# Flamingo-style block: the experts' down projection in three half-precision products

## The chip, the cores and the metric

The kernel runs on one core of one Trainium2 chip. Time is device time in microseconds (us) of one execution, the median of several runs. The engines are TensorE (PE, its weight loads PEld), VectorE (DVE), ScalarE (ACT), GpSimd (POOL) and SyncE (SP, which only issues DMAs here).

## The reference

Two layers on 4096 tokens (64 sequences of 64) of width 128. Each layer is an attention step and then a mixture of experts, each added to x behind a gate:

```
x = x + tanh(g_xattn[0]) * L0_xattn(layernorm(x), ctx)
x = x + tanh(g_ffn[0])   * L0_ffn(layernorm(x))
x = x + tanh(g_xattn[1]) * L1_xattn(layernorm(x), ctx, mask)
x = x + tanh(g_ffn[1])   * L1_ffn(layernorm(x))
```

Layer 0's experts: a router picks the top 2 of 8 experts for a token; for expert e, `h = relu(x @ W1[e] + b1[e])` (128 to 512), `y = h @ W2[e] + b2[e]` (512 to 128), and the two y are added with the router's softmax weights. Layer 1's experts: the 8192 pairs of token and expert are sorted by expert and cut into 8 equal chunks, `h = gelu(x @ w1[e])`, `y = h @ w2[e]`, weighted and added back. Everything is fp32.

## The kernel before

Before each expert stage the tokens' rows are scattered to DRAM (`xs`), sorted by expert. A row holds the normalised token twice in half precision (a high part and the rest, the low part), then its index and its weight. The stage then works through tiles of 256 rows: 40 tiles in layer 0 (an expert's rows are padded to whole tiles) and 32 in layer 1. A round is 8 tiles (`XS_LEAD`). The first and the last round are written out; those between, three in layer 0 and two in layer 1, are a loop with a register for its index. All engines run their own instruction streams and meet by semaphores; buffers and semaphores come in pairs, used by even and odd tiles (`v = q % 2`).

For one tile q:
- SyncE loads two blocks of 128 rows from `xs` (`load_rows`).
- TensorE, `gather`: waits for the rows and transposes them, 4 matmuls of 128x128 in half precision into PSUM (line 929).
- VectorE, `parts`: copies the transposed high and low parts to `xgT` (line 1614).
- TensorE, `up`: 12 matmuls of 256 columns in half precision (line 758, as for all matmuls by `mm`). w1 was split before into `w1h` and `w1l`, scaled by 256 (`WSCALE`); the three products w1h x high, w1h x low and w1l x high are added in PSUM.
- ScalarE, `step`: in layer 0 four Relu activations with a bias (line 1195), in layer 1 one Gelu of 128x1024 (line 1198), out of PSUM to `hid` in fp32, times 1/256.
- TensorE, `down`: for each half u of the tile (128 rows) four fp32 matmuls, with 128 columns of `hid` as weights and the expert's `w2` moving (lines 947 to 950). An fp32 matmul is recorded as two passes.
- VectorE, `result`: waits for y; in layer 0 it loads the expert's number (line 1626) and adds b2; then two multiplications by the rows' weights (line 1632) write `yrow`.
- GpSimd, `step`: a tiny operation `turn` (line 526), then two indirect DMAs that scatter the rows to `ys` (line 528).

The order on TensorE is gather(q+1), up(q), down(q-1); on VectorE parts(q+1), result(q-1). Each instruction stream is in order. Which expert a tile belongs to is known at run time only: `expert(tile)` on TensorE (line 954) loads it from SBUF into a register before each up and each down projection, and the addresses in `w1h`, `w1l` and `w2` are computed from that register by operations of TensorE's sequencer. In the profile these are `PEldq TENSOR_LOAD`, `PEldq FUSED_REGOPS` and `PEldq ALU_OP`; the operations for a matmul's address carry the matmul's line, 758. ScalarE and VectorE load it too in layer 0 (lines 1193 and 1626).

`w2` is loaded once in each layer. In layer 1 the first six tiles are gathered by GpSimd's indirect DMAs (`head_gathered`), the later ones by SyncE.

Of the kernel before, what the change touches and what calls it, by code (L numbers as in the profile page):

```python
# [11 lines left out]
ALU = mybir.AluOpType  # L12
# [9 lines left out]
P = 128  # L22
# [47 lines left out]
def build(nc, A, out):  # L70

    ctx = ExitStack()
    with ctx:
# [154 lines left out]
        hid = at(10.25, [2, FC, TILE])  # L228
        yrow = at(18.5, [XS_LEAD, 2, D])
# [30 lines left out]
        def banks(b, n):  # L260
# [21 lines left out]
              for l in range(2)]  # L282
# [8 lines left out]
        w2_in = sem("w2_in")  # L291
# [5 lines left out]
               ("stored", XS_LEAD), ("biased", 1))}  # L297
# [156 lines left out]
        def _(pool):  # L454
# [41 lines left out]
            g.memset(g32, 0.0)  # L496
# [257 lines left out]
        def _(pe):  # L754
# [157 lines left out]
            def experts(l):  # L912
                f, i0 = ff, before[l]
                pe.wait_ge(w1_lo[l], E)
                if l == 1:
                    pe.wait_ge(w2_in, 16)
# [25 lines left out]
                def down(i, q, e):  # L942
                    v, m = q % 2, (i + i0) * (XS_LEAD // 2) + q // 2
                    pe.wait_ge(f["hid"][v], m + 1)

                    wait(pe, f["yrow"][v], m)
                    for u in range(2):
                        for c in range(FC):
                            ins = mm(PS[:, 6 + v, u * D:(u + 1) * D], hid[:, v, c, u * P:(u + 1) * P],
                                     w2[:, ds(e * FF + c * D, D)], start=c == 0, stop=c == FC - 1)  # L950
                    ins.then_inc(f["y"][v], 1)
# [172 lines left out]
        def _(act):  # L1124
# [58 lines left out]
            def experts(l):  # L1183
                f, i0 = ff, before[l]
                act.wait_ge(table, l + 1)
                act.wait_ge(w_late, 16 * NL)
                def step(i, q):
                    v, m = q % 2, (i + i0) * (XS_LEAD // 2) + q // 2
                    act.wait_ge(f["up"][v], m + 1)
                    wait(act, f["y"][v], m)  # L1190
                    b = 2 + 2 * v
                    if l == 0:
                        e = act.value_load(eidx_i[0:1, l, ds(i * XS_LEAD + q, 1)], min_val=0, max_val=E - 1)
                        for c in range(FC):
                            ins = a.activation(hid[:, v, c, :], PF[:, b * 512 + c * TILE:b * 512 + (c + 1) * TILE],  # L1195
                                               ACT.Relu, bias=b1[:, ds(e * FC + c, 1)], scale=1 / WSCALE)
                    else:
                        ins = a.activation(hid[:, v, :, :].rearrange("p c n -> p (c n)"), banks(b, 1024),  # L1198
                                           ACT.Gelu, scale=1 / WSCALE)
                    ins.then_inc(f["hid"][v], 1)  # L1200

                expert_tiles(act, l, step)
# [84 lines left out]
        def _(dve):  # L1287
# [54 lines left out]
            def load(c):  # L1342
# [5 lines left out]
                if c == 0:  # L1348
# [6 lines left out]
                    dve.wait_ge(gates, 1)  # L1355
                    v_.tensor_copy(wqqa[:, 0:H], PS[:, 4, 0:H])
# [250 lines left out]
            def experts(l):  # L1607
# [9 lines left out]
                def result(i, q):  # L1617
# [3 lines left out]
                    if not (isinstance(i, int) and i + i0 == 0):  # L1621
                        dve.wait_ge(f["turn"][0], (i + i0 - 1) * XS_LEAD + q + 1)
                        dve.wait_ge(f["stored"][q], (i + i0) * STORED)
# [10 lines left out]

                def round_(i, first, last):
                    for q in range(XS_LEAD):
                        if q < XS_LEAD - 1:
# [3 lines left out]
                        if q >= 1:  # L1641
                            result(i, q - 1)
                        elif not first:
                            result(i - 1, XS_LEAD - 1)
# [6 lines left out]
                round_(rounds_ - 1, False, True)  # L1651
                result(rounds_ - 1, XS_LEAD - 1)

# [10 lines left out]
            dve.wait_ge(x1_done, NC)  # L1664
            v_.memset(kmask[:, 0, :, :, :], 0.0).then_inc(k_blank, 1)
# [76 lines left out]
            route_table(1)  # L1742
            experts(1)
# [50 lines left out]
```

## Time and profile before

| | |
|---|---|
| median of 3 runs | 770.82 us (767.83 to 771.95) |
| profiled execution, own time | 765.61 us |
| its span | 763.8 us |
| mean granted TensorE clock | 0.795 of full speed |
| PE busy | 518.3 us, 68% of the span |
| PEld busy | 428.3 us, 56% |
| DVE busy | 416.7 us, 55% |
| ACT busy | 235.4 us, 31% |
| POOL busy | 339.5 us, 44% |
| chain that ended last | PE 50%, DVE 24%, POOL 8%, issue 8%, DMA 6% |
| of it, PE on line 758 | 46% |

The span is the time from the first to the last instruction of the program in the profile. The chain that ended last is followed back from the last instruction, at each step to what released it. Shares of busy time are averages over stages with different limits: the expert stages lie at about 205 to 350 us (layer 0) and 614 to 740 us (layer 1).

### The profile page before, as it was taken

How to read it: one execution, taken by the hardware profiler on the slowest of the kernel's cores; microseconds unless marked ns; L12 is line 12 of the kernel's file. 1: busy time of each engine (PE TensorE's matmuls, PEld its weight loads, DVE VectorE, ACT ScalarE, POOL GpSimd, SP SyncE). 2: the span in 40 equal slices, each digit the busy share in tenths (PEclk: the TensorE clock that was granted, in tenths of full speed). 3: DMA queues.
4: the chain of work that ended last, by engine and by line, in shares of the span. 5: the costliest groups of instructions: out<-in, count | busy, mean ns of one | idle time of the engine just before them, and what ended most of it. 6: DMA issues, size and time to landing. Idle time of an engine off the chain costs nothing.

```text
span 763.8 us, 17097 instructions
## 1 busy us (share of the span) xinstructions
PE 518.3 (68%) x5273; PEld 428.3 (56%) x5274; DVE 416.7 (55%) x1454; ACT 235.4 (31%) x411; POOL 339.5 (44%) x424
## 2 busy tenths in 40 slices
PE   1587958423199999992387687777862076999950
PEld 1255745301199899991254466666651065989950
DVE  4785686987123333334895377878568611222215
ACT  0221011222044444443621365454631021232310
POOL 6212106777345656665500000071647676666650
PEclk9978876755599999997565599696765578999995
DMA  7911101124222222342763265353214123232219
GB/s 210 264 32 42 28 1 44 51 95 129 69 72 79 76 79 73 80 136 76 236 187 124 55 162 151 96 150 71 67 45 147 45 54 101 80 79 80 68 52 317
DMA packets 73194, 76.51 MB, mean 100 GB/s; under 512 B 12984, under 2 KB 61368, under 8 KB 73064
## 3 DMA queue, kind: packets, MB, share of 16 engines
q1 hardware_dynamic: 58504, 50.98, 24.4%
q0 software_dynamic: 10224, 22.40, 9.5%
q10 hardware_dynamic: 4400, 2.26, 1.0%
q8 instruction: 40, 0.66, 0.4%
q14 instruction: 26, 0.21, 0.1%
HBM read 46.15 MB, written 29.34 MB: 99 GB/s over the span
## 4 chain that ended last, share of the span: by engine, by line
PE 50%; DVE 24%; POOL 8%; issue 8%; DMA 6%; ACT 2%; SPq 1%; POOLq 0%; ACTq 0%; DVEq 0%
PE PS L758 46%; POOL xs L517 5%; DVE XN L1323 3%; DVE stats L1302 3%; DMA work<-ys 3%; DVE X L1297 2%; PE PS L929 2%; DVE work L1712 2%; DVE work L1297 1%; POOL work L565 1%; DVE rtmp L1297 1%; DVE mv L1305 1%; DVE nwt L1297 1%; PE PS L1074 1%; DMA work<-max_rows 1%
## 5 line engine op out<-in xcount | busy, mean ns | idle before, releaser
L517 POOL DMA_INDIRECT xs<-pack,adr_i x80 | 78.7, 983 | 197.8 <-ACT pack L1147 142.0
L528 POOL DMA_INDIRECT ys<-work x144 | 140.7, 977 | 34.5 <-issue 34.5
L758 PE MATMUL PS<-w,work 128*128 x1152 | 143.8, 279 | 3.0 <-issue 1.7
L758 PEld LDWEIGHTS PS<-w,work 128*128 128x128 f32 x1152 | 134.9, 193 | 9.0 <-issue 6.8
L758 PE MATMUL PS<-work,w1h 128*128 128x256 f16 x576 | 103.1, 281 | 1.1 <-issue 1.1
L1195 ACT ACTIVATE work<-PS,b 128x256 f32<-128x256 f32 x160 | 62.7, 474 | 95.5 <-PE PS L758 69.2
L1297 DVE TENSOR_TENSOR work<-PS,work 128x256 f32<-128x256 f32 (+3 forms) x82 | 33.0, 405 | 94.7 <-issue 55.6
L758 PE MATMUL PS<-work 97*64 97x256 f16 (+5 forms) x608 | 74.0, 318 | 15.4 <-DVE work L1429 7.6
L758 PE MATMUL PS<-work,w1l 128*128 128x256 f16 x288 | 80.9, 281 | 0.0
L758 PEld LDWEIGHTS PS<-work 97*64 97x64 f16 (+2 forms) x608 | 56.0, 163 | 25.9 <-DVE work L1429 10.9
L1632 DVE TENSOR_SCALAR work<-PS,work 128x128 f32<-128x128 f32 x64 | 19.5, 346 | 79.0 <-PE PS L758 79.0
L929 PE MATMUL PS<-ident,work 128*128 128x128 f16 x288 | 29.5, 228 | 47.2 <-DMA work<-xs,headadr_i 24.6
L758 PEld LDWEIGHTS PS<-work,w1h 128*128 x576 | 54.7, 101 | 8.4 <-issue 2.1
L1712 DVE TENSOR_REDUCE work<-PS 128x16 f32<-128x1024 f32 x32 | 39.1, 1222 | 33.8 <-PE PS L758 33.8
L1198 ACT ACTIVATE work<-PS 128x1024 f32<-128x1024 f32 x32 | 32.8, 1024 | 80.2 <-PE PS L758 80.1
L758 PE MATMUL PS<-work,W 128*128 128x512 f32 x60 | 48.4, 933 | 8.1 <-DVE work L1297 3.4
L517 POOL DMA_INDIRECT xs<-work,adr_i x48 | 47.1, 981 | 14.8 <-issue 13.6
L1614 DVE COPY work<-PS 128x512 f16<-128x512 f16 x72 | 30.1, 418 | 39.7 <-PE PS L929 39.5
L929 PEld LDWEIGHTS PS<-ident,work 128*128 128x128 f16 x288 | 22.8, 102 | 50.7 <-issue 39.6
L526 POOL TENSOR_TENSOR turn<-lane 1x1 f32<-1x1 f32 x72 | 17.3, 240 | 72.6 <-DVE work L1632 72.4
L1236 ACT ACTIVATE XN<-PS,mask_bias 128x1024 f32<-128x1024 f32 x32 | 35.6, 1113 | 19.1 <-PE PS L758 18.9
L758 PE MATMUL PS<-ident,work 128*64 128x36 f32 x512 | 25.9, 255 | 22.7 <-DVE work L1297 22.7
(259 smaller groups left out, 809.8 us busy)
## 6 DMA issues: line engine op xcount, KB each, us to landing
work<-xs SPq DMA_DIRECT2D x132, 65.0 KB
work<-ys SPq DMA_DIRECT2D x12, 512.0 KB, 5.9
k_parts<-work SPq DMA_DIRECT2D x24, 128.0 KB
w<-k_parts SPq DMA_DIRECT2D x8, 384.0 KB
work<-k_parts SPq DMA_DIRECT2D x32, 96.0 KB
work<-q_parts SPq DMA_DIRECT2D x8, 384.0 KB
work<-q_parts SPq DMA_DIRECT2D x32, 96.0 KB
ys<-work POOLq DMA_INDIRECT x144, 2.3
```

The lines of the kernel that those rows point to most:

```text
L517: g.indirect_dma_start(xs[l], bass.IndirectOffsetOnAxis(adr_i[:, k, T:T + 1], 0), pack_of(l, c)[:, s, k, :].bitcast(U32), None)\
L528: g.indirect_dma_start(ys[l], bass.IndirectOffsetOnAxis(xin[:, q, u, :].bitcast(U32)[:, D:D + 1], 0), yrow[:, q, u, :], None).then_inc(ff[ ...
L758: return t.matmul(o, lhsT, rhs, start=start, stop=stop, skip_group_check=True)
L929: ins = t.transpose(o[:, h, u, :], xin[:, q, u, h * D:(h + 1) * D], ident16[:])
L1195: ins = a.activation(hid[:, v, c, :], PF[:, b * 512 + c * TILE:b * 512 + (c + 1) * TILE], ACT.Relu, bias=b1[:, ds(e * FC + c, 1)], scale=1 ...
L1198: ins = a.activation(hid[:, v, :, :].rearrange("p c n -> p (c n)"), banks(b, 1024), ACT.Gelu, scale=1 / WSCALE)
L1236: a.activation(pexp[:, T % 2, :], banks(2, 1024), ACT.Exp, bias=mask_bias[:, T:T + 1]).then_inc(p_done, 1)
L1297: return v_.tensor_tensor(o, x, y, op)
L1302: ins = v_.bn_stats(stats[:, T, :], X[:, T, 0:D])
L1323: ins = v_.tensor_scalar(XN[:, slot + s, :], X[:, T, 0:D], mv[:, T, 0:1], rstd[:, T:T + 1], ALU.subtract, ALU.mult)
L1614: v_.tensor_copy(xgT[:, v, :, :].rearrange("p h n -> p (h n)"), PS[:, v, 0:TILE].bitcast(F16))\
L1712: v_.tensor_reduce(rmaxq[:, c % 2, s, :], banks(0, 1024).rearrange("p (h k) -> p h k", h=H), AX, ALU.max).then_inc(s_max, 1)
```

## The change

The down projection is made like the up projection. `w2` is split into a high and a low half-precision part, times 256, in `w2_parts` (which lies over `XN`): the high parts by ScalarE, 8 copies of 128x512, the low parts by VectorE, 8 operations (`split_w2`), before each expert stage. Behind its activation ScalarE writes `hid_hi`, a half-precision copy of `hid`, in one activation of 128x1024. VectorE makes `hid_lo` = hid - hid_hi in two halves of a tile, 128x512 each (`low`). The down projection has 24 matmuls of 128 columns in half precision: for each half u 8 with `hid_hi` (high and low weights), then, behind a wait for that half of the low part, 4 with `hid_lo` and the high weights. The factor 1/256 goes into the gates' columns `gt[:, 2:4]`, and b2 is multiplied by 256.

VectorE's order in a round becomes result(q-2), parts(q+1), low(q-1); in layer 1's first round low(3) comes before parts(5). ScalarE waits for the low part of tile q-2 before it writes `hid` again, and for the down projection of q-2 before it writes `hid_hi`. The semaphore `turn` starts at 8. The wait for w2 in layer 1 moves from TensorE to ScalarE.

```diff
+        hid_hi = at(48, [2, FC, TILE], F16)
+        hid_lo = at(68, [2, FC, TILE], F16)
+        w2_parts = XN[:].rearrange("p t d -> p (t d)").bitcast(F16)
...
-            g.memset(g32, 0.0)
+            g.memset(g32, 0.0).then_inc(ff["turn"][0], XS_LEAD)
...
                 def down(i, q, e):
-                    v, m = q % 2, (i + i0) * (XS_LEAD // 2) + q // 2
-                    pe.wait_ge(f["hid"][v], m + 1)
+                    v, m, tile = q % 2, (i + i0) * (XS_LEAD // 2) + q // 2, (i + i0) * XS_LEAD + q
+                    if q == 0 and isinstance(i, int) and i == 0:
+                        pe.wait_ge(w2_lo, (l + 1) * E)
+                    pe.wait_ge(f["hi"][0], tile + 1)
 
                     wait(pe, f["yrow"][v], m)
                     for u in range(2):
+                        o = PS[:, 6 + v, u * D:(u + 1) * D]
                         for c in range(FC):
-                            ins = mm(PS[:, 6 + v, u * D:(u + 1) * D], hid[:, v, c, u * P:(u + 1) * P],
-                                     w2[:, ds(e * FF + c * D, D)], start=c == 0, stop=c == FC - 1)
+                            for part in range(2):
+                                mm(o, hid_hi[:, v, c, u * P:(u + 1) * P],
+                                   w2_parts[:, ds(e * 2 * FF + part * FF + c * D, D)], start=c + part == 0, stop=False)
+                        pe.wait_ge(f["lo"][0], 2 * tile + u + 1)
+                        for c in range(FC):
+                            ins = mm(o, hid_lo[:, v, c, u * P:(u + 1) * P],
+                                     w2_parts[:, ds(e * 2 * FF + c * D, D)], start=False, stop=c == FC - 1)
                     ins.then_inc(f["y"][v], 1)
...
             def experts(l):
                 f, i0 = ff, before[l]
+                act.wait_ge(w_late, 16 * NL)
+                act.wait_ge(pack_lo, (l + 1) * NC)
+                if l == 1:
+                    act.wait_ge(w2_in, 16)
+                for e in range(E):
+                    a.activation(w2_parts[:, e * 2 * FF:e * 2 * FF + FF], w2[:, e * FF:(e + 1) * FF], ACT.Copy,
+                                 scale=WSCALE).then_inc(w2_hi, 1)
                 act.wait_ge(table, l + 1)
...
                 def step(i, q):
                     act.wait_ge(f["up"][v], m + 1)
-                    wait(act, f["y"][v], m)
+                    if not isinstance(i, int) or tile >= 2:
+                        act.wait_ge(f["lo"][0], 2 * tile - 2)
...
                     ins.then_inc(f["hid"][v], 1)
+                    act.wait_ge(f["hid"][v], m + 1)
+                    wait(act, f["y"][v], m)
+                    a.activation(hid_hi[:, v, :, :], hid[:, v, :, :], ACT.Copy).then_inc(f["hi"][0], 1)
...
+                    v_.tensor_scalar(gt[:, 2:4], gt[:, 2:4], 1 / WSCALE, None, ALU.mult)
...
+                def low(i, q):
+                    v, m = q % 2, (i + i0) * (XS_LEAD // 2) + q // 2
+                    dve.wait_ge(f["hi"][0], (i + i0) * XS_LEAD + q + 1)
+                    wait(dve, f["y"][v], m)
+                    for u in range(2):
+                        half = slice(u * P, (u + 1) * P)
+                        tt(hid_lo[:, v, :, half], hid[:, v, :, half], hid_hi[:, v, :, half], ALU.subtract)
+                            .then_inc(f["lo"][0], 1)
+
                 def round_(i, first, last):
                     for q in range(XS_LEAD):
+                        if q >= 2:
+                            result(i, q - 2)
+                        elif not first:
+                            result(i - 1, XS_LEAD + q - 2)
+                        late = first and l == 1 and q == HEAD0 - 1
+                        if late:
+                            low(i, q - 1)
                         if q < XS_LEAD - 1:
                             parts(i, q + 1)
                         elif not last:
                             parts(i + 1, 0)
                         if q >= 1:
-                            result(i, q - 1)
+                            if not late:
+                                low(i, q - 1)
                         elif not first:
-                            result(i - 1, XS_LEAD - 1)
+                            low(i - 1, XS_LEAD - 1)
...
+            def split_w2(l):
+                for e in range(E):
+                    hi, lo = (w2_parts[:, (2 * e + part) * FF:(2 * e + part + 1) * FF] for part in range(2))
+                    dve.wait_ge(w2_hi, l * E + e + 1)
+                    v_.scalar_tensor_tensor(out=lo, in0=w2[:, e * FF:(e + 1) * FF], scalar=WSCALE, in1=hi,
+                                            op0=ALU.mult, op1=ALU.subtract).then_inc(w2_lo, 1)
...
             dve.wait_ge(x1_done, NC)
+            dve.wait_ge(w_late, 16 * NL)
+            split_w2(0)
+            v_.tensor_scalar(b2b, b2b, WSCALE, None, ALU.mult)
...
             route_table(1)
+            split_w2(1)
             experts(1)
```

## Rows read from the trace of the kernel before

**Rows 1.** Busy time by stretch, both loops (us, PE, PEld, DVE, ACT, POOL, PEclk, DMA share, GB/s)

```profile
235.00:318.00 83.00, 81.95 (x768) 76.09 (x768) 29.95 (x96) 37.51 (x97) 50.96 (x73) 1.00 0.29 77
653.00:708.00 55.00, 54.47 (x514) 50.84 (x514) 15.13 (x48) 16.37 (x16) 34.05 (x49) 1.00 0.29 78
```

**Rows 2.** Line 929's transposes, two stretches (count: ns min/median/max, first and last start)

```profile
L929 PE MATMUL PS<-ident,work x98: 218/220/220, 235.0 to 318.3; 128*128 128x128 f16 x98
...
L929 PE MATMUL PS<-ident,work x65: 218/220/220, 653.0 to 708.0; 128*128 128x128 f16 x65
```

**Rows 3.** TensorE in order of time, one tile of layer 0 (start, us, engine, line)

```profile
299.39 0.27 PE L758 MATMUL PS<-work,w1l 128*128 128x256 f16 x1
...
299.50 1.97 PE L758 MATMUL PS<-w,work 128*128 x16
...
301.31 0.39 PE L929 MATMUL PS<-ident,work 128*128 128x128 f16 x4
...
302.84 1.95 PE L758 MATMUL PS<-w,work 128*128 x16
...
304.63 0.39 PE L929 MATMUL PS<-ident,work 128*128 128x128 f16 x4
```

**Rows 4.** TensorE's sequencer by line, five successive stretches from 299.3 to 303.0

```profile
L758 PEldq FUSED_REGOPS  x4: 46/46/46, 299.3 to 299.7; - x4
...
L954 PEldq TENSOR_LOAD <-eidx_i x1: 304/304/304, 300.1 to 300.1; - x1
...
L758 PEldq FUSED_REGOPS  x4: 46/46/46, 300.9 to 301.6; - x4
...
L954 PEldq TENSOR_LOAD <-eidx_i x1: 302/302/302, 301.8 to 301.8; - x1
...
L758 PEldq FUSED_REGOPS  x4: 46/46/46, 302.6 to 303.0; - x4
```

**Rows 5.** TensorE in order of time, layer 1's first tiles (idle before, and releaser)

```profile
636.57 0.40 PE L929 MATMUL PS<-ident,work 128*128 128x128 f16 x4 [2.45 <-DMA work<-xs,headadr_i]
640.33 0.61 PE L929 MATMUL PS<-ident,work 128*128 128x128 f16 x4 [3.36 <-DMA work<-xs]
```

**Rows 6.** TensorE's sequencer, line 954, from 639.0 to 640.6

```profile
L954 PEldq TENSOR_LOAD <-eidx_i x1: 395/395/395, 640.3 to 640.3; - x1
```

**Rows 7.** ScalarE and VectorE in order of time, the same tile of layer 0

```profile
300.41 1.57 ACT L1195 ACTIVATE work<-PS,b 128x256 f32<-128x256 f32 x4 [1.76 <-PE PS L758]
...
302.49 0.42 DVE L1297 TENSOR_TENSOR work<-PS,work 128x256 f32<-128x256 f32 x1 [2.02 <-issue]
...
303.35 0.42 DVE L1614 COPY work<-PS 128x512 f16<-128x512 f16 x1
```

**Rows 8.** VectorE in order of time, before each expert stage

```profile
182.39 1.28 DVE L1297 TENSOR_TENSOR work<-PS,work 128x512 f16<-128x512 f32 x2
...
205.24 0.42 DVE L1614 COPY work<-PS 128x512 f16<-128x512 f16 x1 [12.64 <-PE PS L929]
...
614.22 0.42 DVE L1614 COPY work<-PS 128x512 f16<-128x512 f16 x1 [8.51 <-PE PS L929]
```

**Rows 9.** TensorE and VectorE in order of time, one tile of layer 1

```profile
643.84 2.71 PE L758 MATMUL PS<-w,work 128*128 x16
...
646.59 0.61 DVE L1632 TENSOR_SCALAR work<-PS,work 128x128 f32<-128x128 f32 x2 [5.20 <-PE PS L758]
...
647.12 0.42 DVE L1614 COPY work<-PS 128x512 f16<-128x512 f16 x1
```

**Rows 10.** Groups by line (count, busy us, mean ns of one, idle before)

```profile
L528 POOL DMA_INDIRECT ys<-work x144 | 140.7, 977 | 34.5 <-issue 34.5
...
L1147 ACT ACTIVATE pack<-pack 128x1024 f16<-128x1024 f16 x10 | 10.3, 1049 | 5.1 <-DVE pack L1297 5.1
```

**Rows 11.** Busy time by stretch, two in layer 1's attention (columns as in rows 1)

```profile
452.00:456.00 4.00, 2.19 (x61) 1.64 (x57) 3.00 (x6) 2.33 (x4) 0.00 (x0) 1.00 0.80 142
520.00:580.00 60.00, 41.46 (x714) 33.17 (x704) 41.51 (x174) 26.14 (x50) 25.68 (x27) 0.70 0.32 85
```

More of the change, by code:

```diff
@@ L290, in build @@
         w1_in = [[sem(f"w1_in{l}_{u}") for u in range(2)] for l in range(2)]
-        w2_in = sem("w2_in")
+        w2_in, w2_hi, w2_lo = sem("w2_in"), sem("w2_hi"), sem("w2_lo")
         pack_hi, pack_lo = sem("pack_hi"), sem("pack_lo")
@@ L296, in build @@
               (("xin", XS_LEAD), ("xT", 2), ("xT_sb", 2), ("up", 2), ("hid", 2), ("y", 2), ("yrow", 2), ("turn", 1),
-               ("stored", XS_LEAD), ("biased", 1))}
+               ("stored", XS_LEAD), ("biased", 1), ("hi", 1), ("lo", 1))}
         rounds = [TILES[l] // XS_LEAD for l in range(2)]
@@ L914, in experts @@
                 pe.wait_ge(w1_lo[l], E)
-                if l == 1:
-                    pe.wait_ge(w2_in, 16)
                 pe.wait_ge(table, l + 1)
@@ L1184, in experts @@
                 f, i0 = ff, before[l]
+                act.wait_ge(w_late, 16 * NL)
[5 more added lines that the diff above has]
+                                 scale=WSCALE).then_inc(w2_hi, 1)
                 act.wait_ge(table, l + 1)
-                act.wait_ge(w_late, 16 * NL)
                 def step(i, q):
-                    v, m = q % 2, (i + i0) * (XS_LEAD // 2) + q // 2
+                    v, m, tile = q % 2, (i + i0) * (XS_LEAD // 2) + q // 2, (i + i0) * XS_LEAD + q
                     act.wait_ge(f["up"][v], m + 1)
-                    wait(act, f["y"][v], m)
+                    if not isinstance(i, int) or tile >= 2:
+                        act.wait_ge(f["lo"][0], 2 * tile - 2)
                     b = 2 + 2 * v
@@ L1621, in result @@
                     if not (isinstance(i, int) and i + i0 == 0):
-                        dve.wait_ge(f["turn"][0], (i + i0 - 1) * XS_LEAD + q + 1)
+                        dve.wait_ge(f["turn"][0], (i + i0) * XS_LEAD + q + 1)
                         dve.wait_ge(f["stored"][q], (i + i0) * STORED)
@@ L1633, in result @@
                     ins.then_inc(f["yrow"][v], 1)
+                def low(i, q):
[4 more added lines that the diff above has]
+                        half = slice(u * P, (u + 1) * P)
+                        tt(hid_lo[:, v, :, half], hid[:, v, :, half], hid_hi[:, v, :, half], ALU.subtract)                            .then_inc(f["lo"][0], 1)
                 def round_(i, first, last):
                     for q in range(XS_LEAD):
+                        if q >= 2:
[5 more added lines that the diff above has]
+                            low(i, q - 1)
                         if q < XS_LEAD - 1:
@@ L1651, in experts @@
                 round_(rounds_ - 1, False, True)
+                result(rounds_ - 1, XS_LEAD - 2)
+                low(rounds_ - 1, XS_LEAD - 1)
                 result(rounds_ - 1, XS_LEAD - 1)
+            def split_w2(l):
[4 more added lines that the diff above has]
+                                            op0=ALU.mult, op1=ALU.subtract).then_inc(w2_lo, 1)
             def combine(l, c):
```

## The prediction

> **What bounds the kernel now.** I read the expert stages alone, since both layers' down projections lie there. First the busy time by stretch: in the loops TensorE is busy for 81.95 of 83 us in layer 0 and 54.47 of 55 in layer 1, at a granted clock of 1.00 [rows 1]. Then the transposes that open each tile, four to a tile: 24 tiles of layer 0's loop take 83.2 us (235.0 to 318.2), 3.47 us each, and the 16 of layer 1 take 55.0 (653.0 to 708.0), 3.44 each [rows 2]. Then one tile in the order of time [rows 3]: transposes and the up projection (12 matmuls) from 301.31 to 302.84, the down projection from 302.84 to the next transposes at 304.63. So the array's turn is 1.53 + 1.79 = 3.32 us, and the reader sees no hole in it.
>
> A page of busy time can't show the second limit. The rows of TensorE's sequencer [rows 4] are of register work alone: four address operations for a down projection (299.3 to 299.7), a load of the expert's number at 300.1, the operations of an up projection (of eight, the four FUSED_REGOPS are shown, from 300.9), a load at 301.8, the next down's first operation at 302.6. That is 3.3 us for a tile (I take 3.27). The views show nothing that it waits for in between, so the sequencer is about as full as the array. A register operation takes about 0.12 us of it: four starts span 0.4 us with their matmuls between. The matmuls themselves are cheap in it: between the last address operation at 299.7 and the load at 300.1 lie five matmuls, four transposes, a wait and an operation, so a matmul costs at most 0.03. And the sequencer stops at a wait: at 640.33 a transfer releases the transposes [rows 5], and the load behind them in the program starts at 640.3 and not before [rows 6].
>
> **The change, part by part.** *The array.* Eight fp32 matmuls, recorded as 16 passes, take 1.79 us. 24 matmuls of 128 columns in half precision replace them. The nearest row is the four transposes, of the same shape and type and each with its weights loaded: they take 0.39 us with the last one's 0.22 [rows 2, 3], so they start 0.056 apart, and 24 take 1.34. The turn falls from 3.32 to 2.87. Bounds: 0.056 a matmul, and the 0.11 of a pass (1.79 / 16) if loading weights showed beside so short a stream: 2.7 us, a turn of 4.2.
> The Trainium skill, "TensorE: Matmul & The Clock Gate", section "Back-to-back issue gap", gives about 81 ns for a matmul of 128 columns in a stream of loads and matmuls. By it the down projection would take 1.94 us and the turn would be 3.47. The trace has 56 ns, but for four in a row only.
>
> *TensorE's sequencer.* The weights' offset hangs on the expert's register. Today four address operations serve eight matmuls, since the second half of a tile uses the four again. Now there are eight offsets (two parts, four chunks), used again by the low products and by the second half: 4 more operations, 0.48 us. The 16 more matmuls cost 0 to 0.5 at 0.03 each; I take 0.1, since nine matmuls and other work fit into 0.4 above. In the loops the thresholds of the waits differ from tile to tile, one for "hi" and two for "lo": three operations of about 0.1, 0.3. Sum: 3.27 + 0.48 + 0.1 + 0.3 = 4.15, say 4.2 us. In the first and last rounds, which are written out, indices and thresholds are constants, and I estimate 3.75. Bounds: nothing (3.3, all of it cached and free), and an operation for each of the 24 matmuls (4.2 + 16 x 0.12 = 6.1). These turns don't run ahead of anything: the wait for the last low part stops the sequencer, and gather, two loads, the up projection and the next down come behind it.
>
> *VectorE's ring.* low(q-1) stands behind result(q-2) and parts(q+1); result(q-2) needs down(q-2), and down(q-1) needs low(q-1): one turn a tile. In layer 0 the down projection ends at 299.50 + 1.97 = 301.47, but the add of the bias starts at 302.49, since the expert's number is loaded behind the wait; the copy of parts ends at 303.35 + 0.42 = 303.77 [rows 3, 7]. That is 2.30. Two subtractions of 128x512 come on: a pair of such operations takes 1.28 [rows 8], and as VectorE's records overlap by 0.08 I count 1.20. Then a semaphore and the last four matmuls, 0.39 as for four transposes [rows 3] and 0.1 for the first load: 0.53. The turn is 2.30 + 1.20 + 0.53 = 4.03 us. In layer 1 the down ends at 643.84 + 2.71 = 646.55 and the copy at 647.12 + 0.42 = 647.54 [rows 9]: 0.99 + 1.20 + 0.53 = 2.72 us. The subtraction has one fp32 and one half-precision input from SBUF. Bounds: the 0.42 of the half-precision copy of 512 [rows 7], which makes layer 0's turn 3.5, and the pair's 0.69 each, which I take as the nearer in type.
>
> *ScalarE* gets a copy of 128x1024, 1.05 [rows 10], behind 1.57 of activations, which start at 300.41, 0.75 behind the last up matmul (299.39 + 0.27) because of its own load [rows 3, 7]: 3.4, under the 4.0. *GpSimd* issues two scatters of 0.98 for a tile [rows 10], some 2.6 with the gaps: hidden. *The split of w2* is 8 copies on ScalarE and 8 operations of about 0.6 on VectorE, 5 us in each layer, and the scaling of b2 about 1. VectorE is idle for 12.64 us before layer 0's first copy and 8.51 before layer 1's [rows 8], which hides them; without that cover they cost 6 and 5. The scaling of two gate columns is one small operation, 0.2 at most.
>
> *The sum,* against the profiled run's 765.6 us. What today's periods have above the array's turn, at most 0.15 (3.47 against 3.32: the branch, late loads), I add to the longest new turn in the loops: 4.35. Layer 0: 24 x (4.35 - 3.47) = +21.1. Layer 1: 16 x (4.35 - 3.44) = +14.6. Tiles of written-out rounds: 12 in layer 0 at VectorE's 3.95 (its load has less to compute there) against some 3.37, +7; 9 in layer 1 at 3.85 against some 3.4, +4. Filling layer 0's pipeline and draining both: a copy of 1.05 and subtractions of 1.2 come on, less 0.45 of down projection, 3 x 1.8 = +5.4. Layer 1's first tiles run into waits for transfers that end at 636.57 and 640.33 [rows 5]; of the 2.8 us or so that they lose I count 0.4. Together +52.5: 818.1. The median of the runs shown is 5.2 above the profiled run (770.8 against 765.6): about 822 us, that is 823.3 rounded towards the near rivals.
>
> **The rivals.**
> 1. *The array alone is the limit.* Register work and semaphores hide, the turn is 2.87, and 61 tiles save 0.45 or so each: 27.5 us, less the 5.4 of the ends: 770.8 - 22 = 749. For it: rows 1 and 3 show an array without holes. Against it: rows 4, whose turn is 3.3 by itself. It decides from the point where the mean turn falls below some 3.4. This is the faster case.
> 2. *VectorE's ring without the sequencer.* If the sequencer's additions are half of what I think or less, layer 0 runs at 4.03 + 0.1 and layer 1 at 3.4 as now: 24 x 0.66 + 12 x 0.58 + 6 = +29, about 800. If its turn goes below the array's, layer 1 gains some 10 (790), and the subtraction's lower bound takes 36 x 0.5 = 18 from layer 0 (772).
> 3. *Short matmuls run slower in a stream than in fours.* Halfway between the bounds, at 0.083 each and with nothing else new, the turn is 1.53 + 2.0 = 3.5: 61 x 0.18 + 5.4 = +16, about 787. Beneath a sequencer's turn of 4.2 it changes nothing. The figure of "TensorE: Matmul & The Clock Gate" in the Trainium skill, above, would come out here.
> 4. *An address operation for every matmul.* 61 x 1.9 above the forecast, about 938. Against it: four serve eight today.
> 5. *The clock falls.* The array would be busy 2.87 of 4.2 us, 68%. A stretch with 2.19 of 4 busy has a clock of 1.00, while one with 41.46 of 60 has 0.70, there with long holes [rows 11]. Mine are near 1.3 us and regular. At 1.2 GHz the turn is 5.7: 61 x 1.4 more, about 907.
>
> **How the numbers follow.** Forecast 0.63, rival 1 0.07, rival 2 0.19, rival 3 0.04, rival 4 0.04, rival 5 0.03. The range goes from 780, low in rival 2, to 850 (turns of 4.8 in the loops, with 16 matmuls at 0.03 and late loads), and leaves out rivals 1, 4 and 5 and thin ends, under 0.2. A difference within 0.5% can't be told from none here. Faster 0.08 (rival 1 and the bottom of 2), the same 0.03, slower 0.89.
>
> **What would show it.** The transposes of successive tiles 4.2 to 4.4 us apart in both loops, the clock near 1.00, TensorE busy about 70%; eight FUSED_REGOPS for each down projection; VectorE waiting little before its result in layer 0 and over 1 us in layer 1. If layer 1's tiles come 3.3 us apart or less, the sequencer's price is wrong; if layer 0's do, the ring is wrong too. Subtractions of other than 0.69 us, or half-precision matmuls more than 0.06 apart where nothing waits, would shift the terms above.

## The result, and the profile after

The changed kernel takes 821.13 us (median of 4 runs, 815.88 to 824.47), the kernel before beside it 771.38 (4 runs). The ratio is 1.0648, 95% interval 1.0573 to 1.0724: 6.5% slower. The profiled run is of 815.88 us with a span of 813.7, against 765.61 and 763.8 before, so 49.9 us of span have to be found. Of all the runs told below one stands apart: the kernel with fewer thresholds took 1553.8 us in one of its six executions, which no row explains, and its median without it is 817.2 us. In the changed kernel the transposes are on line 930, the matmuls' helper on 761, VectorE's two-tensor helper on 1317, the expert's load on 963.

Busy time by stretch, both loops (columns as in rows 1):

```profile
242.00:328.00 86.00, 75.52 (x798) 58.95 (x796) 47.95 (x119) 51.67 (x100) 49.00 (x61) 1.00 0.23 63
694.00:740.00 46.00, 40.20 (x419) 31.39 (x419) 23.29 (x55) 21.84 (x22) 26.63 (x33) 1.00 0.22 59
```

TensorE was busy for 99% of these stages [rows 1]; now it is for 87 to 88%. That is more than the array's work: a matmul's record is longer (0.22 us) than its place in the stream (0.056 us), so matmuls that start one by one count in full. By the distance of the starts the array has work for 2.87 us of 4.31, 67%. The clock is still 1.00. The transposes that open the tiles, with the first and last start in a window (as in rows 2), of the first loop, the second loop, and the last written-out tiles:

```profile
L930 PE MATMUL PS<-ident,work x100: 218/219/227, 242.9 to 346.5; 128*128 128x128 f16 x100
...
L930 PE MATMUL PS<-ident,work x66: 218/219/220, 684.7 to 753.8; 128*128 128x128 f16 x66
...
L930 PE MATMUL PS<-ident,work x27: 218/219/220, 753.7 to 777.5; 128*128 128x128 f16 x27
```

The 24 tiles of layer 0 take 103.5 us, 4.31 each (before 3.47), the 16 of layer 1 take 69.0, 4.31 each (before 3.44). Six written-out tiles take 23.6, 3.94 each. What fills a tile of layer 1 is on TensorE's sequencer. Four lines of it within one turn, 734.8 to 739.1 (the first is of the down projection alone, to 735.85):

```profile
L761 PEldq FUSED_REGOPS  x8: 46/46/60, 734.8 to 735.7; - x8
...
L956 PEldq FUSED_REGOPS  x1: 42/42/42, 735.8 to 735.8; - x1
L956 PEldq ALU_OP  x1: 32/32/32, 736.0 to 736.0; - x1
...
L963 PEldq TENSOR_LOAD <-eidx_i x2: 303/306/308, 736.3 to 738.2; - x2
...
L947 PEldq ALU_OP  x1: 32/32/32, 738.8 to 738.8; - x1
```

There are eight address operations, 0.12 us apart, where four were [rows 4]; two thresholds for "lo" (line 956) and one for "hi" (line 947); and two loads of the expert's number (line 963). TensorE and VectorE in order of time there:

```profile
734.91 2.06 PE L761 MATMUL PS<-XN,work 128*128 x24 [0.33 <-issue]
736.81 0.39 PE L930 MATMUL PS<-ident,work 128*128 128x128 f16 x4
...
739.15 0.48 PE L761 MATMUL PS<-XN,work 128*128 x3 [0.35 <-issue]
```
```profile
732.91 0.61 DVE L1653 TENSOR_SCALAR work<-PS,work 128x128 f32<-128x128 f32 x2 [1.98 <-PE PS L761]
...
733.77 1.28 DVE L1317 TENSOR_TENSOR work<-work 128x512 f16<-128x512 f32 x2
737.01 0.61 DVE L1653 TENSOR_SCALAR work<-PS,work 128x128 f32<-128x128 f32 x2 [1.96 <-PE PS L761]
```

TensorE has holes put down to "issue", and VectorE waits 1.96 us for it: layer 1's turn, 734.91 to 739.15, is the sequencer's. In layer 0 VectorE is in it too:

```profile
300.39 0.42 DVE L1317 TENSOR_TENSOR work<-PS,work 128x256 f32<-128x256 f32 x1 [1.93 <-PE PS L761]
300.85 0.48 DVE L1653 TENSOR_SCALAR work<-work 128x128 f32<-128x128 f32 x2
301.24 0.42 DVE L1635 COPY work<-PS 128x512 f16<-128x512 f16 x1
301.58 1.28 DVE L1317 TENSOR_TENSOR work<-work 128x512 f16<-128x512 f32 x2
304.44 0.42 DVE L1317 TENSOR_TENSOR work<-PS,work 128x256 f32<-128x256 f32 x1 [1.57 <-PE PS L761]
```
```profile
L345 PEldq EVENT_SEMAPHORE  x1: 51/51/51, 302.9 to 302.9; - x1
...
L963 PEldq TENSOR_LOAD <-eidx_i x1: 303/303/303, 303.2 to 303.2; - x1
```

The second subtraction ends at 301.58 + 1.28 = 302.86; TensorE's sequencer passes its next wait at 302.9 and starts the load behind it at 303.2. In layer 1 the load comes 1.2 us after the subtraction instead (736.3, against 733.77 + 1.28 = 735.05). VectorE's turn from result to result is 304.44 - 300.39 = 4.05 us here. It is one of the short ones: the next takes 4.39, and the loop's turns go from 4.01 to 4.79 round the mean of 4.31.

### The profile page after: what moved, and what is told of

The parts are those of the page before. It is cut to its first block, busy times and chain, and to the rows that moved or that the text cites. A ratio compares the mean times of both kernels' runs of the same rounds, so it can differ in the third digit from the quotient of the medians.

```text
span 813.7 us, 19014 instructions
## 1 busy us (share of the span) xinstructions
PE 538.4 (66%) x5849; PEld 411.4 (51%) x5850; DVE 512.9 (63%) x1616; ACT 319.4 (39%) x499; POOL 367.6 (45%) x424
## 4 chain that ended last, share of the span: by engine, by line
PE 50%; DVE 24%; issue 10%; POOL 6%; DMA 6%; ACT 1%; SPq 1%; DVEq 0%; POOLq 0%; ACTq 0%
PE PS L761 46%; POOL xs L520 3%; DVE XN L1343 3%; DVE stats L1322 3%; DMA work<-ys 2%; DVE X L1317 2%; PE PS L930 2%; DVE work L1317 2%; DVE work L1761 2%; DVE rtmp L1317 1%; POOL work L568 1%; DVE mv L1325 1%; DVE nwt L1317 1%; PE PS L1083 1%; POOL work L575 1%
## 5 line engine op out<-in xcount | busy, mean ns | idle before, releaser
L761 PE MATMUL PS<-XN,work 128*128 (+1 forms) x2752 | 174.1, 232 | 27.2 <-issue 22.7
L531 POOL DMA_INDIRECT ys<-work x144 | 165.1, 1146 | 34.3 <-issue 34.3
L761 PEld LDWEIGHTS PS<-XN,work 128*128 128x128 f16 (+1 forms) x2752 | 137.6, 103 | 72.6 <-issue 54.5
L1317 DVE TENSOR_TENSOR work<-work 128x512 f16<-128x512 f32 (+2 forms) x160 | 100.8, 667 | 6.2 <-ACT work L1220 5.6
L1220 ACT ACTIVATE work<-work 128x1024 f16<-128x1024 f32 x72 | 76.1, 1057 | 2.3
L761 PEld LDWEIGHTS PS<-work,w1h 128*128 x576 | 51.9, 100 | 26.2 <-issue 18.9
L930 PEld LDWEIGHTS PS<-ident,work 128*128 128x128 f16 x288 | 19.8, 101 | 49.6 <-issue 42.2
```

Source lines behind the costliest of these rows:

```text
L531: g.indirect_dma_start(ys[l], bass.IndirectOffsetOnAxis(xin[:, q, u, :].bitcast(U32)[:, D:D + 1], 0), yrow[:, q, u, :], None).then_inc(ff[ ...
L761: return t.matmul(o, lhsT, rhs, start=start, stop=stop, skip_group_check=True)
L930: ins = t.transpose(o[:, h, u, :], xin[:, q, u, h * D:(h + 1) * D], ident16[:])
L1220: a.activation(hid_hi[:, v, :, :], hid[:, v, :, :], ACT.Copy).then_inc(f["hi"][0], 1)
L1317: return v_.tensor_tensor(o, x, y, op)
```

## The experiments

Twelve kernels, in three sets, each with runs of the kernel before on the same chip (median 767.6, 767.1 and 767.2 us). The table has each ratio to these, which can differ by 0.2% from the quotient of the medians. The changed kernel was timed beside the kernel before in its own set only, so it is compared with the others by its ratio, and by its tiles. From each profiled run the table has the mean tile in the two loops (start of tile 9's transposes to tile 33's, and 49's to 65's) and in the last written-out tiles (33 to 39, 65 to 71).

| kernel | us | ratio [95%] | loop 0 | loop 1 | written out 0 / 1 |
|---|---|---|---|---|---|
| before | | 1 | 3.47 | 3.44 | 3.42 / 3.37 |
| changed | 821.1 | 1.065 [1.057, 1.072] | 4.31 | 4.31 | 4.21 / 3.94 |
| constant address | 790.7 | 1.031 [1.025, 1.037] | 4.00 | 3.19 | 3.90 / 3.11 |
| early load on VectorE | 814.9 | 1.062 [1.057, 1.068] | 4.21 | 4.32 | 3.97 / 3.94 |
| one load | 799.0 | 1.043 [1.036, 1.050] | 4.14 | 3.80 | 4.03 / 3.34 |
| one load + early load | 790.0 | 1.031 [1.025, 1.037] | 3.90 | 3.78 | 3.82 / 3.36 |
| the same + ScalarE's early | 784.8 | 1.021 [1.014, 1.029] | 3.72 | 3.78 | 3.59 / 3.36 |
| one subtraction | 834.8 | 1.086 [1.079, 1.094] | 4.52 | 4.23 | 4.41 / 3.92 |
| fewer thresholds | 817.6 | 1.068 [1.062, 1.073] | 4.27 | 4.08 | 4.19 / 3.87 |
| expert from the number | 771.5 | 1.003 [1.000, 1.007] | 3.71 | 3.00 | 3.59 / 2.87 |
| all edits | 767.7 | 1.001 [0.998, 1.005] | 3.66 | 2.98 | 3.59 / 2.87 |
| before, one load | 764.9 | 0.998 [0.994, 1.002] | 3.35 | 3.36 | 3.32 / 3.32 |
| before, third load | 810.1 | 1.058 [1.050, 1.065] | 4.13 | 4.14 | 4.08 / 4.00 |
| before, number | 763.6 | 0.995 [0.992, 0.999] | 3.35 | 3.32 | 3.32 / 3.32 |

**Constant address.** The down projection's weights stand at a fixed address, one load less. This kernel leaves out the choice of the expert there (every tile takes expert 0's `w2`):

```
-    w2_parts[:, ds(e * 2 * FF + part * FF + c * D, D)]      (and the same for the low part)
+    w2_parts[:, part * FF + c * D:part * FF + c * D + D]
-    down(i, q - 1, expert(i * XS_LEAD + q - 1))
+    down(i, q - 1, 0)
...
```

> The changed kernel, but every down projection uses expert 0's weights: its expert load and its eight address operations on TensorE's sequencer are gone, the 24 matmuls and all waits stay. Theory (sequencer sets layer 1, VectorE's ring sets layer 0): the sequencer's turn falls by 8 x 0.12 + 0.75 us; layer 1's tiles come some 2.95 us apart (array 2.87), layer 0's stay at the ring's 4.0 to 4.1; about 787 us against 821. Rival A (24 short matmuls run slowly on the array): layer 1 stays at 4 us or more, 815 us or more. Rival B (the chain activation, copy, subtraction sets both layers): no tile moves, 821 us.

+24 us against the kernel before instead of +50. Layer 1 falls to 3.19 us a tile, below the kernel before's 3.44, with all 24 matmuls in place: what the change cost there is address work and loads, not matmuls. (2.95 was expected; what holds it at 3.19 is open.) Layer 0 stops at 4.00, and there VectorE's ring is alone in charge:

```profile
294.06 0.42 DVE L1317 TENSOR_TENSOR work<-PS,work 128x256 f32<-128x256 f32 x1 [1.49 <-PE PS L761]
...
298.03 0.42 DVE L1317 TENSOR_TENSOR work<-PS,work 128x256 f32<-128x256 f32 x1 [1.49 <-PE PS L761]
```

Every turn from result to result in this loop is between 3.94 and 4.08 us, with 1.47 to 1.60 between the last subtraction and the next result. The forecast's 0.53 for the semaphore and the last matmuls and 1.02 from there to the add (302.49 - 301.47) are 1.55.

**Early load on VectorE.** The load of the expert's number in `result` goes ahead of the wait for y:

```
+    if l == 0:
+        e = dve.value_load(eidx_i[0:1, l, ds(i * XS_LEAD + q, 1)], ...)
     dve.wait_ge(f["y"][v], m + 1)
...
     if l == 0:
-        e = dve.value_load(eidx_i[0:1, l, ds(i * XS_LEAD + q, 1)], ...)
```

> The changed kernel, but VectorE loads the expert's number of layer 0 before it waits for y, not behind the wait. Theory: the ring of layer 0 falls from 4.03 to some 3.3 us, but the sequencer's 4.2 stands beside it in the loops, and its 3.8 in the written-out rounds; only 3 to 6 us are gained, about 817 us, layer 1 unmoved. Rival B (VectorE's ring alone sets layer 0, the sequencer nothing): 0.75 us on each of 38 tiles, 28 us, about 793.

Layer 0's loop gains 0.10, its written-out tiles 0.24. VectorE's ring alone isn't the bound: its rival had 0.75 a tile.

**One load.** TensorE keeps the register from up(q) for down(q). At the first tile of a round, where the down projection is of the round before, it still loads twice:

```
-    up(i, q, expert(i * XS_LEAD + q))
+    e = expert(i * XS_LEAD + q)
+    up(i, q, e)
     if q >= 1:
-        down(i, q - 1, expert(i * XS_LEAD + q - 1))
+        down(i, q - 1, e_before)
...
+    e_before = e
```

> The changed kernel, but TensorE loads the expert's number once a tile (kept in its register from the up projection to the down projection) and not twice. Theory: the sequencer's turn falls by some 0.7 us to 3.5; layer 1's tiles come 3.5 to 3.6 us apart (from 4.23), layer 0's stop at the ring's 4.05; about 799 us. Rivals A (array) and B (VectorE's ring or the chain of activations alone): no change, 821 us.

As expected in time. Layer 1 gains 0.51 of the 0.7 us in the loop and 0.60 outside; layer 0, which VectorE holds too, 0.17. Turn by turn its trace is plainer than its mean: from result to result, 20 of the loop's 23 turns take 3.96 to 4.21 us, most of them 3.96 to 4.03, as with the constant address, and three, one to a round, where the second load is left, take 4.9 to 5.2.

**One load and early load,** both edits:

> Both edits together: one load a tile on TensorE, and VectorE's load before its wait. Theory: two limits side by side in layer 0, so the two together give more than the sum of each alone; layer 0 at 3.5 to 3.6 us a tile, layer 1 at 3.5 to 3.6; about 781 us. If only one of the two limits existed, the time would be that of the better single edit.

790 and not 781: layer 0 gives 0.41 a tile, more than the two apart (0.10 + 0.17), but stops at 3.90. A third ring was under it. ScalarE, its load (line 1212 on its sequencer), then TensorE, of this kernel:

```profile
267.99 1.57 ACT L1214 ACTIVATE work<-PS,b 128x256 f32<-128x256 f32 x4 [1.25 <-DVE work L1319]
269.59 1.06 ACT L1222 ACTIVATE work<-work 128x1024 f16<-128x1024 f32 x1
```
```profile
L1212 ACTq TENSOR_LOAD <-eidx_i x1: 277/277/277, 267.4 to 267.4; - x1
```
```profile
266.89 0.27 PE L761 MATMUL PS<-work,w1l 128*128 128x256 f16 x1
267.00 1.96 PE L761 MATMUL PS<-XN,work 128*128 x24
...
270.80 2.09 PE L761 MATMUL PS<-XN,work 128*128 x24
```

The up projection ends at 267.16, the activations start 0.83 later, the copy to half precision ends at 270.65, and the down projection of the same tile starts at 270.80: 3.64 us. The profile puts the 0.83 down to VectorE, but ScalarE's load of the expert's number starts at 267.4, right behind the up projection's end, and the activations behind that. In the 3.64 us TensorE does one turn's work (down, transposes, up), so they bound the turn: the down projections here start 3.80 apart.

**The same with ScalarE's load early** (its `value_load` goes ahead of the wait for up):

> The changed kernel with one expert load a tile on TensorE and with the loads of VectorE and ScalarE in layer 0 put ahead of their waits for TensorE (the earlier run had the first two of these; it was 22 us slower than the kernel before). Theory (what kept that run's layer 0 at 3.90 us was the chain TensorE's up projection, ScalarE's load of 0.7 us, its activations 1.57, its copy 1.06, then TensorE's next down projection, 3.6 us with the semaphores, with one up projection a turn): without the load the chain is 2.9 us and the sequencer sets the turn as in layer 1, 3.78 in the loop and about 3.45 in the written-out rounds: 24 x 0.12 + 12 x 0.37 = 7 us less, 15 us slower than the kernel before, between 12 and 18. Rival (the sequencer or VectorE held layer 0): no change from that run, 20 to 24 us slower than the kernel before.

Layer 0 falls from 3.90 to 3.72 in the loop and from 3.82 to 3.59 outside, while layer 1, where ScalarE loads nothing, stays at 3.78 and 3.36. The third ring is shown.

**One subtraction** for the whole tile in place of two halves, one wait:

```
-    pe.wait_ge(f["lo"][0], 2 * tile + u + 1)
+    if u == 0:
+        pe.wait_ge(f["lo"][0], 2 * tile + 2)
...
-    for u in range(2):
-        half = slice(u * P, (u + 1) * P)
-        tt(hid_lo[:, v, :, half], ...).then_inc(f["lo"][0], 1)
+    tt(hid_lo[:, v, :, :], hid[:, v, :, :], hid_hi[:, v, :, :], ALU.subtract).then_inc(f["lo"][0], 2)
```

> The changed kernel with one edit: the low part of a tile is made by one subtraction of 512 elements a partition, not by two of 256, and TensorE waits for it once, after the first half's products with the high part, so one threshold less is worked out by its sequencer. Theory (the sequencer sets the turn, the halves buy nothing): 0.16 to 0.3 us less of the sequencer's 4.15 us, of which layer 0 keeps a part because VectorE's ring, 4.0 us, stands just under it: 16 x 0.2 in layer 1's loop, 9 x 0.1, and 24 x 0.15 in layer 0's: 7 us less than the changed kernel, 43 us slower than the kernel before, between 39 and 49. Rival (the halves matter: the array waits for the whole low part 0.6 us longer, and VectorE's ring of result, low part and down projection grows by it): 0.3 to 0.6 us more in each of layer 0's tiles, 12 to 24 us slower than the changed kernel.

Theory and rival were each right in one layer. Layer 1, the sequencer's, gains 0.08 a tile; layer 0, VectorE's, loses 0.21. TensorE and then VectorE in layer 0:

```profile
283.28 1.19 PE L761 MATMUL PS<-XN,work 128*128 x8 [0.29 <-issue]
284.76 1.07 PE L761 MATMUL PS<-XN,work 128*128 x16 [0.29 <-DVE work L1318]
```
```profile
283.49 1.22 DVE L1318 TENSOR_TENSOR work<-work 128x1024 f16<-128x1024 f32 x1
```

16 matmuls wait for the subtraction's end at 284.71, where only the last four would. The halves of the change are worth their price. But 36 x 0.2 - 16 x 0.08 is 6 us, and this kernel's median is 18 us above what the changed kernel's ratio gives (767.1 x 1.065 = 817). The profiled runs lie further apart than the medians, 24.7 us of span (838.4 against 813.7). Of these, 11 us lie between the layers and 5 ahead of layer 0's first transposes (211.4 against 206.2), where nothing was edited. The stretch between the layers:

```profile
388.00:667.00 279.00, 165.89 (x2444) 127.95 (x2444) 193.86 (x668) 111.94 (x176) 90.19 (x85) 0.69 0.39 111
```
```profile
375.00:643.00 268.00, 159.74 (x2446) 125.07 (x2445) 193.51 (x671) 112.07 (x177) 88.51 (x85) 0.71 0.41 116
```

The first row is of this kernel, the second of the changed one: the same instructions, a mean clock of 0.69 against 0.71, and 11 us. From the last tile of layer 0 to the first of layer 1, the profiles here have 272 to 285 us. Whether the end of layer 0 sets how this stretch fares wasn't tried. So I read small edits by their tiles.

**Fewer thresholds.** A semaphore for each half, all three waits on tile + 1:

```
-    pe.wait_ge(f["lo"][0], 2 * tile + u + 1)
+    pe.wait_ge(f["lo"][u], tile + 1)
...
```

> The changed kernel with one edit: the low part's two halves count in two semaphores, so that the three waits of a down projection (high part, first and second half of the low part) have one threshold, tile + 1, and TensorE's sequencer works out one number a tile where it worked out three. Nothing else moves. Theory (the sequencer sets layer 1's turn; in layer 0 VectorE's ring stands at 4.0 us just under it): 0.25 us less in layer 1's loop, 4.05, and 0.1 to 0.2 less in layer 0's, 4.15; 16 x 0.25 + 24 x 0.15 = 8 us less than the changed kernel, 42 us slower than the kernel before, between 38 and 47. Rival (the ring through VectorE or the matmuls set the turn): no change, 50 us slower.

By its tiles the theory held: 0.23 in layer 1's loop (0.25 expected), 0.04 in layer 0's, where the sequencer then waits for VectorE. The time doesn't show it: the tiles give 24 x 0.04 + 16 x 0.23 = 4.6 us, and the stretch between the layers was 5 us longer in this profile.

**The expert from the tile's number,** in layer 1, on top of the three loads' edits (each expert has four tiles there):

```
 def expert(tile, of=None):
+    if l == 1:
+        return of[0] * (XS_LEAD // 4) + of[1] // 4
...
```

> The kernel with one expert load a tile on TensorE and early loads on VectorE and ScalarE (18 us slower than the kernel before), with one more edit: in layer 1, where the tile's number gives its expert, TensorE's sequencer works the expert out from the number and loads nothing. Theory (the sequencer sets layer 1's turn, 3.78 us in the loop and 3.36 outside it; without the load it is 3.0, and the array's 2.87 us of matmuls with a short gap behind them comes next): 3.2 in the loop, 3.1 outside, 16 x 0.55 + 9 x 0.25 = 11 us less, 7 us slower than the kernel before, between 3 and 11. Rival (VectorE or ScalarE holds layer 1): no change, 18 us slower than the kernel before.

Layer 1's loop falls to 3.00 us (3.2 was expected), and outside it, where nothing is left for the sequencer to compute, the array's own turn is laid open:

```profile
717.01 0.39 PE L930 MATMUL PS<-ident,work 128*128 128x128 f16 x4
...
718.54 1.50 PE L761 MATMUL PS<-XN,work 128*128 128x128 f16 x24
719.88 0.39 PE L930 MATMUL PS<-ident,work 128*128 128x128 f16 x4
```

1.53 + 1.34 = 2.87 us, 0.056 for each of 24 matmuls. This is the forecast's turn of the array, to the hundredth.

**All edits together:** one load a tile, the early loads on VectorE and ScalarE, layer 1's expert from the tile's number, and fewer thresholds.

> All edits that took instructions from TensorE's sequencer or from the chains of layer 0, together: one expert load a tile, early loads on VectorE and ScalarE, layer 1's expert from the tile's number, one threshold for the three waits. Theory (layer 0: the sequencer, 3.72 us in the loop, falls to 3.45, below it lies VectorE's ring of 3.3; layer 1: the array's 2.87 us, 3.0 to 3.1 measured as a turn, below before's 3.44): 24 x 0.25 + 16 x 0.15 less than the kernel without the thresholds' edit, so about 1 us faster than the kernel before, between 6 faster and 5 slower. Rival (the array's work in the changed kernel is not less than before's): 10 us or more slower than the kernel before.

1 us faster was expected, 1 us slower came, and the interval (-0.2 to +0.5%) holds no difference: a tie, with the changed kernel's 24 matmuls a tile. Layer 1's tiles are now 0.46 shorter than before's, layer 0's still 0.19 longer. There, in some tiles, the sequencer stops 0.6 us at the wait for the second half, and load, addresses and the next up projection come behind it. And the turn in which a round's second load is left takes 4.3 to 4.9 us, where the others take 3.25 to 3.87.

**The kernel before, one load; a third load; number.** The mirror: the same instructions taken from or added to the kernel before. The third load is one line, `expert(i * XS_LEAD + q)`, ahead of up.

> The kernel before, with one edit: the register with a tile's expert number is loaded once a tile on TensorE (nine loads for eight tiles) and kept for the down projection, instead of twice. Theory (array and sequencer nearly tied before, 3.32 us and 3.27 us a tile, and what one gives the other does not take at once: the sequencer's second load falls where the array has emptied its queue): the loops' 3.47 and 3.44 us go down to the array's 3.3, 40 tiles x 0.15 = 6 us, the written-out rounds keep 3.3 to 3.4; about 6 us faster than the kernel before, between 3 and 9. Rival (the array alone sets the tile's turn before): no change, within 1.5 us. Rival (sequencer alone): the loops fall by the whole 0.7 us a tile or to 2.9: 20 us or more faster.

> The kernel before, with one edit: a third load of the tile's expert number on TensorE's sequencer in each tile, whose value nobody uses. Theory (the sequencer is next to the array and becomes the bound when 0.7 us of instructions are added): 3.27 + 0.7 = 4.0 us a tile in the loops and about 3.7 in the written-out rounds: 24 x 0.53 + 16 x 0.56 + 28 x 0.3 = 30 us slower than the kernel before, between 22 and 38. Rival (the sequencer is hidden behind the array, and the changed kernel is slower for other reasons, its ring through VectorE and its matmuls): within 5 us of the kernel before.

> The kernel before with the same two savings on TensorE's sequencer: one expert load a tile in layer 0, none in layer 1. It leaves the array as the bound, 3.32 us a tile. Theory: 24 x 0.12 + 16 x 0.1 = 4.5 us less than the kernel before, between 1 and 7; layer 1's turn is 3.32 us, since nothing is left to take from the array. Rival (the sequencer held the loops of layer 1 by itself): 3.2 us or less a tile there, 8 us or more faster than the kernel before.

The third load costs 0.66 and 0.70 us a tile in the loops, and 43 us in all. Its theory had 30 and at most 38, with 0.3 for a written-out tile, but those slow by 0.63 to 0.66 as well. Its loop of layer 1:

```profile
L929 PE MATMUL PS<-ident,work x67: 218/219/220, 676.2 to 742.7; 128*128 128x128 f16 x67
```

(16 tiles in 66.3 us.) So before, the sequencer stood right under the array, as rows 4 had it. Taking a load away gives 0.12 and 0.08 a tile and ends just above the array's 3.32, at 3.35 and 3.36. In time 6 us were expected of it, and its 2.2 us can't be told from no change. With layer 1's loads gone too, the loop there is 3.32:

```profile
L929 PE MATMUL PS<-ident,work x67: 219/219/219, 652.9 to 706.2; 128*128 128x128 f16 x67
```

This version is the fastest of all, 0.5% under the kernel before (interval 0.1 to 0.8%).

## Why the prediction was right, step by step

822 us was forecast against 821.1 measured. The mechanism was right. That the number is right to 1 us is in part luck: the sum went by the profiled run, 818.1 against 815.9, in which two misses of some 3 us cancel (below), and that the median lies 5.2 above the profiled run again is chance.

- *The array,* 2.87: shown, in the kernel with the expert from the number. Rival 1 (749 us) fell: the array's turn is what it said, and the sequencer doesn't let it through. Rival 3 fell: a stream of 24 keeps 0.056. The Trainium skill's 81 ns ("TensorE: Matmul & The Clock Gate", section "Back-to-back issue gap") isn't what this trace has, and the measurement decides.
- *The sequencer,* 4.15 to 4.2: eight address operations and three thresholds, as forecast; 4.24 in the turn shown above. Its price was tested from both sides: a load taken away or added moves a tile by 0.5 to 0.7, three thresholds made one by 0.23 (some 0.12 each, 0.1 was taken). Rival 4 (an operation for each matmul) fell by the x8.
- *VectorE's ring,* 4.03 in layer 0: 4.05 in the turn shown. Subtractions cost 0.68 to 0.69 us each, as taken from the pair in rows 8. With the sequencer relieved (constant address) the whole loop runs at 4.00. In layer 1 it was forecast at 2.72: VectorE's result, copy and subtractions take 735.05 - 732.91 = 2.14, with the forecast's 0.53 for the semaphore and the last matmuls 2.67, and it idles 1.96 us before the next result.
- *Which of the two bounds layer 0.* The forecast took the longer and added 0.15. They are coupled, as I read it: the sequencer stops for VectorE's second half, then runs its own work, and VectorE waits for what this leads to. Relieving one gives 0.10 or 0.17, both 0.41, and then ScalarE's ring, which the forecast had at 3.4 without the semaphores and which has 3.64 with them, stands next. Rival 2 would have had VectorE's ring in charge and no more. It fell for the changed kernel, since the sequencer holds layer 1 and has its share in layer 0, but its state of layer 0 can be had: with the address operations and a load gone (constant address) every turn there is VectorE's, and with one load gone most are.
- *The clock* (rival 5) stayed at 1.00 in both loops.
- *Hidden work.* The splits of w2 took 4.91 and 4.90 us, beside an idle VectorE. The first:

```profile
188.07 4.91 DVE L1697 SCALAR_TENSOR_TENSOR XN<-w,XN 128x512 f16<-128x512 f32 x8
...
206.83 0.42 DVE L1635 COPY work<-PS 128x512 f16<-128x512 f16 x1 [8.85 <-PE PS L930]
```

Whether they are hidden wholly isn't shown for layer 0. In the four profiles of the kernel before and its variants the first transposes start at 202.5 to 204.7 us, in the ten with the splits at 204.0 to 211.4, 2.9 later in the mean, and no run took the splits out by themselves.

The terms of the sum, against the 49.9 us of span. A drain is counted from the last tile's transposes to the start of GpSimd's last scatter of that layer; in layer 0 this start is, before and after:

```profile
355.94 0.97 POOL L528 DMA_INDIRECT ys<-work  x1 [0.30 <-issue]
```
```profile
391.47 0.97 POOL L531 DMA_INDIRECT ys<-work  x1 [0.30 <-issue]
```

| term | forecast | measured |
|---|---|---|
| loop of layer 0, 24 tiles | +21.1 | +20.3 |
| loop of layer 1, 16 tiles | +14.6 | +14.0 |
| 12 written-out tiles of layer 0 | +7 | +10.0 |
| 9 of layer 1 | +4 | +3.3 |
| filling, draining, layer 1's first tiles | +5.8 | +5.9 |
| all other | 0 | -3.6 |

Two terms are off, with opposite signs. The written-out tiles of layer 0 take 4.20, not 3.95. Two things were sized too low: the sequencer's turn outside the loops, which in layer 1, where VectorE's ring is short, is 3.94 and not 3.75, and the coupling, which the forecast left out here: the ring it took alone is 3.9 (with one load less these tiles take 3.86 and 4.03, with the constant address 3.87 and 3.90). The other is what was taken at nothing. The changed kernel's profile is 1.6 us longer ahead of layer 0, 4.3 shorter between layer 0's last scatter and layer 1's first transposes, and 0.8 shorter behind the last scatter of all. The long one of these stretches has 253.3 to 264.5 us in the profiles here, the changed kernel's being the shortest of the fourteen, so I read the -3.6 as luck of this run and not as a gain of the change.

Within the terms that fit: the filling is +1.0 and the drains +2.6 and +1.6, against 1.8 each; layer 1's first six tiles are +0.6, against 0.4. Of the 9 tiles of layer 1, the three behind these six run no slower than before (4.16 us against 4.20), and the last six by 0.57 each, not 0.45.

What had no test: why the stretch between the layers moves, what the splits of w2 cost ahead of layer 0, and what layer 0 would take with its address operations gone but its loads in place.

## What to carry to other kernels

Count an engine's register operations, value loads and waits for one turn of the loop before you count its matmuls: in this kernel a full array hid a sequencer just as full, and a change that saves 0.45 us of array a tile cost 0.84 to 0.87. Shorter matmuls with addresses from registers pay only where the addresses and loads don't stand beside them, as in layer 1 without its loads (3.00 us a tile against 3.32 for the kernel before with the same edit). Over the whole kernel all edits together gave a tie here. Three ways to take such work off the path: a value loaded once and kept, computed from the loop's index, or loaded ahead of the wait rather than behind it. Where two rings stand within some tenths of each other, relieve both before you judge either, and give the written-out rounds the coupled turn too.

## What the runs showed of the hardware that was not expected

GpSimd's scatter slows beside VectorE's subtractions. Its groups before and after (columns as in rows 10) have 977 ns [rows 10] and

```profile
L531 POOL DMA_INDIRECT ys<-work x144 | 165.1, 1146 | 34.3 <-issue 34.3
```

In order of time, of the changed kernel and then of the one with one subtraction:

```profile
301.76 1.36 POOL L531 DMA_INDIRECT ys<-work  x1 [0.16 <-issue]
303.42 0.97 POOL L531 DMA_INDIRECT ys<-work  x1 [0.30 <-issue]
```
```profile
283.67 1.89 POOL L531 DMA_INDIRECT ys<-work  x1 [0.16 <-issue]
285.86 0.98 POOL L531 DMA_INDIRECT ys<-work  x1 [0.30 <-issue]
```

The first of a tile's two falls on the subtractions (301.58 to 302.86; 283.49 to 284.71) and takes 1.36 us beside halves, 1.89 beside a whole; the second falls beside none and takes 0.97. With the subtractions of 0.68 and of 1.22 us the delay is 0.39 and 0.91. It seems to be off the path here, since GpSimd waits 1.0 to 1.4 us for VectorE before its next tile in both kernels; no run tests that. The Trainium skill, "SBUF — State Buffer", section "Who interferes with whom", says that an operation of two tensors, both in SBUF, contends with GpSimd's reads, and infers that making descriptors isn't touched by it. These rows agree with the first. They show the issuing instruction itself delayed, and not which of its parts (reading the addresses, or making the descriptors) is held up.

Not expected either: the stretch between the layers, the same instructions each time, takes between 272 and 285 us, at mean clocks from 0.72 down to 0.69. That is more than most of the single edits are worth.
